# Two dense layers with adapters over 2048 tokens: gate and up as Strassen-type products over pairs of tiles, down and the last layer once for all tokens

## The reference, cut to what matters

```
gate = x @ W_gate.T + 0.5 * (x @ A_gate[l0].T) @ B_gate[l0].T     # rank 16, adapter l0 chosen per batch row
up   = x @ W_up.T   + 0.5 * (x @ A_up[l0].T)   @ B_up[l0].T
act  = silu(gate) * up                                            # 2048 x 2752
x1   = x + act @ W_down.T + 0.5 * (act @ A_down[l0].T) @ B_down[l0].T
out  = x1 + x1 @ W_out.T + bias + scale[l1] * (x1 @ A_out[l1].T) @ B_out[l1].T
```

## Time and profile before

| | |
|---|---|
| median of the runs | 1779.84 us (lowest 1777.62) |
| the profiled execution: span, first to last instruction | 1777.8 us |
| TensorE busy | 1731.2 us (97%), 7516 matmuls |
| VectorE busy | 779.0 us (44%) |
| ScalarE busy | 433.8 us (24%) |
| GpSimd busy | 554.7 us (31%) |
| moved by DMA | 100.87 MB, mean 57 GB/s |
| mean granted TensorE clock | 0.992 |

### The profile page before, as it was taken

One profiled execution on the slowest core, in us unless ns is written; L12 is line 12 of the kernel. 1 busy time (PEld: TensorE's weight loads), 2 busy tenths in 40 slices (PEclk: granted clock), 3 DMA queues, 4 the chain that ended last, 5 costly groups with the idle time before them and its releaser, 6 DMA issues. The chain is left out here.

```text
span 1777.8 us, 22774 instructions
## 1 busy us (share of the span) xinstructions
PE 1731.2 (97%) x7516; PEld 1400.7 (79%) x7516; DVE 779.0 (44%) x910; ACT 433.8 (24%) x738; POOL 554.7 (31%) x481
## 2 busy tenths in 40 slices
PE   6999999999999999999979999999999999999998
PEld 5788888888888888868757888888888888888686
DVE  7642432433433423484285424424334334335832
ACT  5412212213113112161053112122131131131610
POOL 5722313213213222152157223232142132131521
PEclk9999999999999999999989999999999999999999
DMA  8302202112112212024263112121122131120232
GB/s 182 90 25 50 58 26 66 49 27 75 49 27 75 48 26 54 15 59 122 51 154 77 37 39 62 26 62 49 27 75 49 27 75 49 26 57 25 54 77 48
DMA packets 225336, 100.87 MB, mean 57 GB/s; under 512 B 148740, under 2 KB 224900, under 8 KB 225284
## 3 DMA queue, kind: packets, MB, share of 16 engines
q1 hardware_dynamic: 191360, 91.85, 21.2%
q10 hardware_dynamic: 33796, 8.39, 2.2%
q0 software_dynamic: 128, 0.00, 0.0%
HBM read 91.79 MB, written 8.39 MB: 56 GB/s over the span
## 5 line engine op out<-in xcount | busy, mean ns | idle before, releaser
L917 PE MATMUL ps<-X,Wk 128*128 128x512 f32 x4960 | 1157.2, 392 | 36.8 <-DVE X L746 27.5
L917 PEld LDWEIGHTS ps<-X,Wk 128*128 128x128 f32 x4960 | 932.9, 188 | 243.9 <-issue 31.7
L917 PE MATMUL ps<-act,Wd 128*128 128x512 f32 (+1 forms) x2080 | 482.9, 391 | 1.9 <-DVE acc L801 1.3
L917 PEld LDWEIGHTS ps<-act,Wd 128*128 128x128 f32 (+1 forms) x2080 | 388.3, 188 | 93.1 <-issue 8.0
L639 POOL TENSOR_TENSOR Wk<-turned,Wk 128x512 fp32r<-128x512 f32 (+2 forms) x220 | 291.8, 1335 | 531.6 <-ACT Wk L471 530.7
L801 DVE TENSOR_TENSOR acc<-acc,ps 128x1024 f32<-128x1024 f32 (+1 forms) x196 | 238.5, 1219 | 255.9 <-PE ps L917 255.8
L639 POOL TENSOR_TENSOR Wd<-turned,Wd 128x512 fp32r<-128x512 f32 (+2 forms) x104 | 128.3, 1271 | 553.4 <-ACT Wd L471 552.7
L765 DVE TENSOR_TENSOR work<-work,ps 128x1024 f32<-128x1024 f32 x42 | 51.3, 1221 | 561.0 <-PE ps L917 560.9
L471 ACT ACTIVATE Wk<-turned 128x512 fp32r<-128x512 f32 (+2 forms) x228 | 136.3, 617 | 470.9 <-PE ps L917 382.5
L484 ACT ACTIVATE act<-work 128x1024 fp32r<-128x1024 f32 x42 | 44.6, 1062 | 515.1 <-PE ps L917 488.0
L705 DVE STREAM_TRANSPOSE turned<-raw 128x1024 f32<-128x1024 f32 (+1 forms) x104 | 123.1, 1198 | 18.9 <-POOL Wd L639 6.1
(11 more groups left out here) (55 smaller groups left out, 441.2 us busy)
## 6 DMA issues: line engine op xcount, KB each, us to landing
raw<-in_L_cond_W_down_dram SPq DMA_DIRECT2D x176, 128.0 KB, 2.9
raw<-in_L_cond_W_gate_dram SPq DMA_DIRECT2D x168, 128.0 KB, 2.5
raw<-in_L_cond_W_up_dram SPq DMA_DIRECT2D x168, 128.0 KB, 2.8
raw<-in_x_dram SPq DMA_DIRECT2D x64, 128.0 KB, 3.0
raw<-in_L_cond_weight_dram SPq DMA_DIRECT2D x64, 128.0 KB, 2.9
out_dram<-work ACTq DMA_DIRECT2D x32, 128.0 KB, 2.4
out_dram<-acc ACTq DMA_DIRECT2D x32, 128.0 KB, 2.5
raw<-in_L_cond_B_gate_dram SPq DMA_DIRECT2D x80, 16.0 KB, 1.8
```

The lines of the kernel that those rows point to most:

```text
L917: return nc.tensor.matmul(dst, stationary, moving, start=start, stop=stop)
```

## The change

It does four things.

First, gate and up of one chunk are computed together. The weights are taken as a 2 x 2 block matrix: rows gate and up, columns the even and the odd k-tiles (A11, A12 of gate, A21, A22 of up). x is a 2 x 2 block matrix too: rows even and odd k-tiles, columns the first and the second 512 tokens of the half. Strassen's method in Winograd's form makes the four results from seven products instead of eight. It needs four sums of weights (S1 to S4) per chunk and four sums of x (T1 to T4) per half.

Second, the seven products accumulate in four PSUM banks; three intermediate values go through SBUF (`p1buf`, `qbuf`, `vbuf`).

Third, the activation of each chunk is stored to memory (`act_scratch`), and x, turned, too (`xt_scratch`). Down runs after both halves, block by block, over all 2048 tokens; then the last layer, over all 2048 tokens.

Fourth, there are no loops: all instructions are written out. RAW is 3. The high and low parts of the weights go into a ring of 4 slots, each with the weights of one product (12 matmuls).

The first loads, in order: x0, x1, G, x4, x5, adapter A, x2, x3, U, x6, x7, adapter A, adapter B (0.5 MB each but the adapters). There are 22 units in a half (21 full tiles and one of 64 + 64 rows), 44 in all.

The core of the diff (the removed part is the kernel above):

```
+USES = {"P1": ["A11"], "P2": ["A12"], "P3": ["S4"], "P4": ["A22"], "P5": ["S1"], "P6": ["S2"], "P7": ["S3"],
+        "A0": ["Ag0"], "A1": ["Ag1"], "C": ["N", "S"], "D": [], "E11": [], "E21": []}
+MOVES = {"P1": "B11", "P2": "B21", "P3": "B22", "P4": "T4", "P5": "T1", "P6": "T2", "P7": "T3"}
...
+        def stages_of(u):
+            if u == 0:
+                return ["P1", "P2", "A0", "P5", "P6", "A1", "P7", "P4", "E11", "E21", "D", "P3"]
+            if u == FULL:
+                return ["P1", "P2", "C"]
+            return ["P1", "P6", "P5", "P7", "P2", "D", "P4", "P3"]
...
+            def product(U, item, region, dst, js=range(KP), start=True, stop=True):
+                slot = ring[w_at[U, item] % RING]
+                for j in js:
+                    for wl, xl in THREE:
+                        last = matmul(dst, slot[:, wl, j, :], XR[region][:, xl, j, :],
+                                      start=start and j == 0 and (wl, xl) == (0, 0),
+                                      stop=stop and j == KP - 1 and (wl, xl) == (1, 0))
+                return last
...
+            def a_product(U, p):
+                h = U // UNITS
+                dst = bank(1, "dc"[p])
+                if U > 0:
+                    eng.wait_ge(c22d_done, full(U - 1))
+                    eng.wait_ge(q_done, U)
+                    eng.wait_ge(v_done, U)
+                item = f"Ag{p}"
+                wait_w_low(eng, U, item)
+                slot = ring[w_at[U, item] % RING][:, :, :, :].rearrange("p l j m -> p (l j m)")
+                regions = (("B11",), ("B21",)) if p == 0 else (("T1", "B11"), ("B22",))
+                for e in range(2):
+                    for kq in range(2):
+                        for region in regions[e]:
+                            wait_x_low(eng, h, region, kq)
+                    for j in range(KP):
+                        k = 2 * j + e
+                        for region in regions[e]:
+                            for l in range(2):
+                                last = matmul(dst, slot[:, k * P:(k + 1) * P], XR[region][:, l, j, :],
+                                              start=(k == 0 and l == 0 and region == regions[0][0]),
+                                              stop=(k == KT - 1 and l == 1))
+                up(U, item.replace("Ag", "A"), last)
...
+            def first_unit(U):
+                a, b, c, d = (bank(U % 2, n) for n in "abcd")
+                free_a(U)
+                up(U, "P1", stage_p(U, "P1", a))
+                eng.wait_ge(p1_done, U + 1)
+                up(U, "P2", stage_p(U, "P2", a, start=False))
+                a_product(U, 0)
+                free_c(U)
+                up(U, "P5", stage_p(U, "P5", c))
+                free_b(U)
+                up(U, "P6", stage_p(U, "P6", b))
+                a_product(U, 1)
+                eng.wait_ge(q_done, U + 1)
+                up(U, "P7", stage_p(U, "P7", b, start=False))
+                eng.wait_ge(v_done, U + 1)
+                up(U, "P4", stage_p(U, "P4", b, start=False))
+                up(U, "E11", adapter(U, 0, 0, a))
+                up(U, "E21", adapter(U, 1, 0, b))
+                free_d(U)
+                up(U, "D", adapter(U, 1, 1, d, start=True))
+                eng.wait_ge(c22_done, full(U))
+                stage_p(U, "P3", c, start=False)
+                up(U, "P3", adapter(U, 0, 1, c))
...
+            def unit(U):
+                a, b, c, d = (bank(U % 2, n) for n in "abcd")
+                free_a(U)
+                up(U, "P1", stage_p(U, "P1", a))
+                free_b(U)
+                up(U, "P6", stage_p(U, "P6", b))
+                free_c(U)
+                up(U, "P5", stage_p(U, "P5", c))
+                eng.wait_ge(q_done, U + 1)
+                up(U, "P7", stage_p(U, "P7", b, start=False))
+                eng.wait_ge(p1_done, U + 1)
+                stage_p(U, "P2", a, start=False)
+                up(U, "P2", adapter(U, 0, 0, a))
+                free_d(U)
+                up(U, "D", adapter(U, 1, 1, d, start=True))
+                eng.wait_ge(v_done, U + 1)
+                stage_p(U, "P4", b, start=False)
+                up(U, "P4", adapter(U, 1, 0, b))
+                eng.wait_ge(c22_done, full(U))
+                stage_p(U, "P3", c, start=False)
+                up(U, "P3", adapter(U, 0, 1, c))
...
+        def _(eng):          # vector
+            def first_unit(U):
+                h = U // UNITS
+                if h == 0:
+                    x_low(h, "T2", 1)
+                else:
+                    second_act(U - 1)
+                turn_ag(("Ag", h, 1))
+                if h == 1:
+                    x_low(h, "T2", 0)
+                    x_low(h, "T2", 1)
+                x_sum(h, "T4", 0)
+                x_sum(h, "T4", 1)
+                x_low(h, "T4", 1)
+                turn_b(("b", h, 0))
+                for w in range(2):
+                    t_sum(h, 0, w)
+                add_q(U)
+                for w in range(2):
+                    t_low(h, 0, w)
+                turn_tile(("G", U + 1))
+                b_low(U)
+                for w in range(2):
+                    t_sum(h, 1, w)
+                turn_tile(("U", U + 1))
+                add_v(U)
+                for w in range(2):
+                    t_low(h, 1, w)
+                sums(U + 1, (1, 2, 3))
+                first_act(U)
+                sums(U + 1, (4,))
+                add_c22(U)
+                b_low(U + 1)
+                add_c12(U)
...
+            def unit(U):
+                h, u = divmod(U, UNITS)
+                second_act(U - 1)
+                add_q(U)
+                turn_tile(("G", U + 1))
+                if u + 1 < FULL:
+                    turn_tile(("U", U + 1))
+                if u % 2:
+                    turn_b(("b", h, (u + 1) // 2))
+                if u + 1 < FULL:
+                    sums(U + 1, (1, 2, 3))
+                else:
+                    sums_half_tile(U + 1)
+                if u in SPILL_UNITS:
+                    turn_x(("y", h, SPILL_UNITS.index(u)))
+                if h == 0 and u == FULL - 1:
+                    x_low(1, "T1", 0)
+                add_v(U)
+                if u + 1 < FULL:
+                    sums(U + 1, (4,))
+                add_c22(U)
+                b_low(U + 1)
+                first_act(U)
...
+                add_c12(U)
...
+        def _(eng):          # scalar
+            def unit(U):
+                h, u = divmod(U, UNITS)
+                silu_second(U - 1)
+                copy_p1(U)
+                w_high(U, "A12")
+                store_act(U - 1)
+                w_high(U, "A22")
+                w_high(U, "S4")
...
+                w_high(U + 1, "A11")
+                b_high(U + 1)
...
+                if u < FULL - 1:
+                    w_high(U + 1, "S2")
+                    silu_first(U)
+                    w_high(U + 1, "S1")
+                    w_high(U + 1, "S3")
...
+        def _(eng):          # gpsimd
+                elif u < FULL - 1:
+                    for item in ("A12", "A22", "S4"):
+                        w_low(U, item)
+                    for item in ("A11", "S2", "S1", "S3"):
+                        w_low(U + 1, item)
...
+        def _(sp):           # sync
+                    elif item == ("D", 0, 1):
+                        load_ad(0)
+                        for k in range(KT):
+                            load_acc(0, k)
+                        load_act(2)
+                        for k in range(KT):
+                            load_acc(1, k)
+                        load_act(3)
...
+        def _(eng):          # vector
+            def down_block(bb):
+                for n, s in enumerate(s for s in B_CLOSE if s[0] == bb):
+                    add_down(s)
+                    if n == 2:
+                        turn_item(("D", bb + 1, 0))
+                    elif n == 4:
+                        turn_item(("D", bb + 1, 1))
+                    elif n == 6:
+                        turn_ad(bb + 1)
...
+        def _(eng):          # scalar, in x_high
+                if name == "T4":
+                    eng.wait_ge(x_sums.sem, x_sums.after((h, "T4", 1)))
+                    eng.wait_ge(x_lo_p.sem, max(x_lo_p.after((h, n, 1)) for n in ("B21", "B22", "T3")))
```

2465 lines of the change are left out of this document (1589 added, 876 removed).

## The result

The changed kernel takes 1748.65 us (median of 4 runs, 1748.49 to 1749.37), the one before 1779.84 us in the same comparison (median of three runs, 1777.62 to 1781.71; a fourth took 2180.05 us and is left out here and in the ratio). The ratio is 0.9828 with a 95% interval of 0.9814 to 0.9843: 1.7% faster, where 3.5% were forecast. The prediction had said that a difference under 2% is what no change would look like, with a chance of 0.20 against 0.74 for faster: by its own mark this is no change. The profiled execution has a span of 1746.8 us. The time lies inside the range given, 1684 to 1766, but 33 us above the forecast of 1716. All lines from here on named L... without a kernel are those of the kernel after.

A forecast was written before the change was run, and what follows sets the result against it. TensorE, 97% busy at 0.2285 us a matmul, was taken as the bound: 7028 matmuls give 1605.9, plus waits 4 + 6 + 52 + 21 + 16 + 3 + 8, makes 1715.9, so 1716 us; range 1684 to 1766.

The forecast's parts named there:

- the half switch: Where the second half of the tokens begins: 21 us lost, 10 of it before P2; ends 12 and 32.
- the end: After the last layer's stream: 8 us lost (7 to 10), the last sum twice as wide and one more.
- the steady unit: Ordinary gate and up unit: 88 matmuls in 20.1 us, no engine full; 4 us charged for VectorE and GpSimd blocking each other.
- the time to spare before P4: In a steady unit: add_v ready 0.25 us early in 8 units with B and the spill, 1.5 or more in others.
- The switch to down: Start of down: TensorE stops at +20 us as W_down queues behind other loads; 16 us lost, ends 3 and 28.
- the first unit: First gate and up unit: VectorE's work and waits put add_q at 65, v_done at 75; 52 us lost, ends 40 and 66.
- down to last layer: Passage from down to the last layer: adapter chain of 8 us under 7 us of matmuls; 3 us lost (0 to 8).
- steady losses: Steady stretches: 4 us for VectorE and GpSimd blocking each other plus 6 us kept from the kernel before.
- Rival (b): Steady unit: VectorE's two-operand passes wait out GpSimd's low parts, 23.4 us a unit instead of 20.1; 1844 us, chance 0.06.
- Rival (a): Whole kernel: serial stretches take nearly all, every term at its upper end; 1791 us, no change; chance 0.17.
- (c): TensorE's stream: matmuls not fewer, or slower in one bank; 1769 us at 236 ns; chance 0.03.
- (d): Starts and switches: better than laid out, giving 1671 us; chance 0.12 for below 1690.

The follow-up runs named there:

- e5_first: Changed kernel with the first unit of each half reordered: T4's low part behind add_q, Ag1 before T3, adapter's first product copied before T4's high parts; 1748.71 us.

## Where the prediction failed and where it was right

The forecast was 63 us less, 1716 for 1779; measured are 31. The matmuls saved are the 111.5 us that it had. What failed is the sum of what goes back into waits and slower matmuls: 110 us forecast, 141 measured. Three terms were too small: the half switch, the switch from down to the last layer, and the end. In them stand two steps that were wrong in kind. VectorE's passes were entered at the length that they have alone, and TensorE's slower matmuls behind a wait (28 us in the whole kernel) had no term at all.

**Right.** The count (7028), the rate and the steady unit (a unit every 20.1 us) stand; the time to spare before P4, 0.25 us in the tight units and 1.5 or more in the others, was 0.06 and 1.14. The switch to down cost 17.0 where 16 were forecast, 13.18 us of it one wait, at 1014 us. The gap came about 20 us into down, with VectorE waiting for W_down, as written.

**Right in sum, in part by luck: the first unit.** vbuf was forecast at 75 and done at 75.9; the loss was forecast at 52 and measured at 54.8. But VectorE's sums for T4 took 3.4 us each instead of 1.2 and the low part of T4 2.6, about 6 us more than entered, and its wait there was 4.4 us in all instead of 7.4, with less waiting elsewhere too: the errors nearly cancel. TensorE's longest waits were 13.9 us at the start and 8.06 us before the second adapter product, for GpSimd's low part of Ag1; before P7, where one of the longest was forecast, it waited 0.93. P4's twelve matmuls took 4.84 us, and the 128th matmul ended at 84.5 us and not at 81. One changed order (e5_first) is all that was tried here, so what sets this unit is read from the trace and not shown.

**Two errors that offset each other in the switch to down.** load_act(2) went out at 989.57, 8.9 us after the switch at 980.67 and not 3.8. From there to the landing of W_down it took 22.3 us and not 25.7, with up to 420 GB/s moved where 285 had been entered. The upper end doesn't come out of its own numbers: 25.7 us at 285 GB/s are 33.4 at 219, 7.7 us more, which makes it 24 and not 28.

**Wrong in size: the half switch, 21 for 35.5.** The step was "P2 starts at 12.9: 10 lost. ... v_done is 7 late. In all 21". The waits were there and in these places: 10.5 for P2, 5.0 before P7, 4.2 before P4. But P2 began 18.6 us after the switch (503.24) and not 12.9, and the loss up to P4 was 30.4 us where 21 were forecast. The passes had been entered at the length that they have alone ("x_low B11 (2)", measured 4.51); the kernel with GpSimd's passes narrowed starts P4 8.4 us earlier and puts that at 8.9 us of the time. Another 2.2 us are P4's matmuls at half clock, for which no term stood, and 3.0 us are two waits of TensorE in the last two units of the first half (0.92 and 2.05). The upper end, 32, was passed as well. The earlier trace rows had shown GpSimd's passes lengthened beside VectorE's and not VectorE's own, so it gave no length to enter; but I had used the lock as a charge on the steady unit, where it was hidden, and as the upper end of the first unit, and left it out of the seam, where it was bare.

**Wrong in size: down to last layer, 3 for 17.** The step was "8 us under 7 us of matmuls". The chain for one pair was about right, 4.61 us of wait. But it came twice, and the second one stood on VectorE in front of additions that free the banks (6.57 us), with 16 transposes for the last layer behind (1.36). These three waits make 12.5 us, and slower matmuls the other 4.4:

```profile
1501.48 2.93 PE L1731 MATMUL ps<-act,Wd 128*128 128x512 f32 x6 [6.57 <-DVE acc L817]
```

Narrowing sum and mask took 5.6 us away, moving them 3.9.

**Wrong in size: the end, 8 for 16.** The step was "the last sum is twice as wide and there is one more". I had overlooked that tile 14's adapter comes behind tile 15's products, so two tiles are finished after the last matmul. Moving it took 5.1 us off the stretch behind the last matmul and 4.3 off the time.

**Too high: 10 for steady losses, measured -2.5.** I had charged 0.5 us in tight units and carried 6 us over from the kernel before. It offset just under a third of the errors.

**The rivals.** Rival (b), the lock in the steady unit, did not cost time: it makes L614, L628 and L456 1.1, 0.5 and 0.7 us longer in each unit, and VectorE's 15.1 us for 12.1 are mostly this. By the forecast's own sum it begins to cost at 7.6 us. The first two stand in places that have cover, L456 in front of vbuf. The experiments say how near it was: one or two short passes more in front of vbuf (0.92 and 1.78 us) cost 17 and 23 us, four (3.86 us) cost 222. Rival (a), everything at its upper end, was half right: three terms passed even those ends (35.5, 17 and 16 against 32, 8 and 10), the others stayed near the forecast or under it. (c) and (d) are excluded by the counts and the table.

## What to carry to other kernels

When matmuls are saved by giving other engines more work, price the seams by the list of the engine that works in order, with each pass at the length that it has beside its neighbour and not alone, and add to the last wait of a few microseconds in a seam the half clock that follows it. An earlier start of the step that waits longest is worth nothing unless the list behind it gets shorter (2 of 10 us at the half switch, 0 of 2 in the first unit). Small loads that an in-order engine needs go ahead of the large ones in the queue: the order alone was worth 14.8 us here, the most of all the edits.

## What the runs showed of the chip that I had not expected

- A VectorE pass of 64 columns with two operands in SBUF took up to 2.44 us beside a GpSimd pass of 2.4; alone it took 0.23. Transposes, and sums that read PSUM, kept their lengths (1.24 and 0.68 us).
- Behind waits of 3.3 to 3.9 us twelve matmuls took 4.2 to 5.5 us instead of 2.93, once 3.02; behind waits of 0.25 to 0.7 us they took 3.0. In between there is no clean order: behind 1.68 us they took 4.60, behind 2.14 us 3.00 (both with the two transposes before vbuf).
- A window of 5 us moved 420 GB/s, where I had worked out 285 from the mean packets; loads of 1 MB landed in 5.0 us (median of 21).
- On ScalarE's queue the 16 stores of 128 KB at the end went out over 10.0 us, mostly 0.5 us each and the rest waiting for the last transposes.
